# Twenty-eight transposes moved from TensorE to the DMA queue, and the whole order written anew, in a decoder layer

## The chip, the cores and the metric

The kernel runs on one core of a Trainium2 chip. The metric is the device time of one execution in microseconds (us), as the median of several runs.

## What is computed

The input is 16 batches of 128 tokens by 256 features. Three stages follow each other, and each ends in a residual sum and a layer norm:

```python
q  = (x @ W_q.T).reshape(B, S, H, hd);  kv = (x @ W_kv.T).reshape(B, S, H, hd)   # H = 16, hd = 16
qf, kvf = l2_normalize(fft(q)), l2_normalize(fft(kv))
values  = ifft(qf * cumsum(kvf, axis=1)).real @ W_o.T
x1 = layernorm(x + values)
x2 = layernorm(x1 + mha(x1, ctx, ctx))          # 16 heads, causal mask before the softmax
x_q = ternary(x2, 0.33, 0.5);  w = ternary(weight, 0.2, 0.6) + rram_variation
out = layernorm(x2 + x_q @ w.T)
```

## The kernel before

Every batch is one tile of 128 partitions (tokens), and all 16 go through the same steps. There is no loop: for each engine the whole program is written out as a list of calls, `step(batch)` or `step(batch, part)`, with waits on semaphores between them. Each engine works its list from top to bottom, so a step that has to wait holds everything behind it on its engine. Steps of up to six batches are mixed in a list. Tables at the top (`PROJ`, `CUM`, `APPROX`, `SCORES`, `OUT` and others) say in which of the eight PSUM banks each product of each batch lies. Most tiles have two buffers, taken by batch number modulo 2.

The steps of one batch, with the engine and the line that the profile gives:

- First stage. `project` (TensorE, L747) makes q and kv in the frequency domain; `square`, `log_norms`, `root_norms`, `square_roots` (ScalarE) and `sum_squares`, `half_step`, `refine_norms`, `unit_vectors` (VectorE) scale them to length one. `cumulate` (TensorE, L753) is the running sum. `straight_products`, `cross_products` (VectorE) and `y_real`, `y_imaginary` (GpSimd, L334, L339) multiply. `transpose_y` and `attend` (TensorE, L759, L767) end the stage.
- Every layer norm i of a batch: the residual sum with its total (`add_attention`, `add_cross_attention` L2028, `add_feed_forward` L2034), `negative_mean` (VectorE, L2040), `deviations` (ScalarE, L1449), `variance` and `root` (GpSimd, L344, L349), then the scaling (`normalise_x1` L2048, `normalise_x2` L2053 on VectorE, `result` for the third).
- Second stage. `round_x1` writes a bfloat16 copy of x1 (tile `x1_b`). `transpose_x1_b` (TensorE, L774) turns it into PSUM, four 128x128 pieces; `copy_x1T_b` brings it back to SBUF (tile `x1T_b`). `approximate` (TensorE, L785) makes rough scores from it, and `row_max` (VectorE, L2067, four parts c) takes their row maxima, which are written into a spare column of x1. Then `transpose_x1` (L792), `copy_x1T` (L1427), `score` (L802) make the exact scores with the maxima already subtracted, `exponentials` (ScalarE, L1431) and `mask` (GpSimd, L355) the weights, `weigh` (TensorE, L809, four parts c) the weighted sums, `copy_outT`, `transpose_out` (L816), `invert_sums`, `divide` (L2077) the result.
- Third stage. `ternary_above` and `ternary` (L2062) make the bfloat16 ternary input `xq`, `transpose_xq` (TensorE, L822) and `copy_xqT` turn it, `feed_forward` (L829) multiplies it with three bfloat16 parts of the weight.

Some steps have two forms, and the lists say for each batch which engine does it: `round_x1` is on ScalarE (L1419) for twelve batches and on VectorE (L1967) for four; `copy_x1T_b` is on ScalarE (L1423) for fifteen and on VectorE (L1971) for one; `copy_xqT` is on ScalarE (L1440) for fourteen and on VectorE (L1975) for two; `result` is on VectorE (L1979) for twelve and on ScalarE (L1444) for four, where it also needs `shift_of` (VectorE, L2044); `ternary_above` is on VectorE (L2058) for eleven and on GpSimd (L360) for five.

`score` and `approximate` use 32 rows of the TensorE array for one product and `weigh` 32 columns, so that several products lie in the array side by side (tiled products); all other products use the whole array. All loads and stores are issued by SyncE (SP) in one list.

## Time and profile before

| | |
|---|---|
| median of 3 runs | 160.67 us (160.65 to 160.75) |
| the profiled execution | 160.63 us, of which the span of the trace is 158.9 us |
| granted TensorE clock, mean over the span | 0.983 |

The profile gives for each engine the busy time within the span, the work that ended last as a chain followed back from the end, the idle time before an instruction and what ended it, and the instructions in order of time. Busy times of TensorE overlap with its own next instruction, so there the distance from one start to the next is the better measure.

### The profile page before, as it was taken

The numbers are of one execution on the slowest core, as the hardware profiler recorded it, in microseconds if no ns is written. First come the engines' busy times: TensorE is split into PE (matmuls) and PEld (weight loads), VectorE is DVE, ScalarE is ACT, GpSimd is POOL, SyncE is SP. The second block draws the span as 40 slices with busy tenths as digits, with TensorE's granted clock in tenths as the row PEclk, the third lists the DMA queues.
The fourth block names the chain that finished last, engine by engine and source line by source line (L and its number), as shares of the span: only waits on it lengthen the run. The fifth ranks groups of instructions, "written<-read, shape, count | busy, mean of one in ns | idle before, by whom it ended". The sixth has DMA issues, their size and how long they took to land.

```text
span 158.9 us, 4915 instructions
## 1 busy us (share of the span) xinstructions
PE 142.3 (90%) x1821; PEld 96.2 (61%) x1821; DVE 140.4 (88%) x428; ACT 117.5 (74%) x320; POOL 99.2 (62%) x210
## 2 busy tenths in 40 slices
PE   6999999999999999899999999987979899978450
PEld 2844566645777766468655767755747667865230
DVE  0148999999999998999989999999999899999872
ACT  3116566567996899956897898897968988988761
POOL 4000256141489178957777971999766998998742
PEclk9999999999999999999999999999999999999985
DMA  4968702398330123503058232032106011020222
GB/s 105 286 197 238 257 8 66 103 294 304 99 103 2 41 95 103 194 8 127 11 182 270 80 101 67 4 102 77 65 0 199 5 37 37 0 70 0 86 78 71
DMA packets 13624, 16.58 MB, mean 104 GB/s; under 512 B 1568, under 2 KB 9504, under 8 KB 13600
## 3 DMA queue, kind: packets, MB, share of 16 engines
q1 hardware_dynamic: 13600, 16.27, 32.5%
q8 instruction: 14, 0.23, 0.6%
q14 instruction: 10, 0.08, 0.2%
HBM read 14.16 MB, written 2.10 MB: 102 GB/s over the span
## 4 chain that ended last, share of the span: by engine, by line
DVE 42%; PE 30%; POOL 12%; ACT 8%; issue 5%; POOLq 0%; DVEq 0%
DVE x L2067 15%; PE p L747 13%; POOL rstd L349 5%; POOL probs L355 4%; PE p L767 3%; PE p L753 3%; DVE x L2048 3%; POOL ve L344 3%; ACT dev L1449 2%; ACT probs L1431 2%; DVE x L2053 2%; PE p L802 2%; PE p L718 2%; DVE xq L2062 2%; DVE r L2028 2%
## 5 line engine op out<-in xcount | busy, mean ns | idle before, releaser
L355 POOL TENSOR_SCALAR_AFFINE_SELECT probs<-probs 128x512 f32<-128x512 f32 x64 | 41.0, 659 | 4.9 <-ACT probs L1431 4.0
L2067 DVE TENSOR_REDUCE x<-p 128x4 f32<-128x512 f32 x64 | 41.2, 681 | 0.0
L1431 ACT ACTIVATE probs<-p 128x512 f32<-128x512 f32 x64 | 34.9, 603 | 4.8 <-PE p L802 4.8
L747 PE MATMUL p<-w_in,xT_s 128*128 128x512 f32 x64 | 30.2, 602 | 0.3 <-ACT w_in L1391 0.3
L349 POOL TENSOR_TENSOR rstd<-ve,power 128x1 f32<-128x1 f32 x48 | 28.2, 588 | 2.3
L1449 ACT ACTIVATE dev<-r,neg 128x256 f32<-128x256 f32 x48 | 24.3, 510 | 3.8 <-DVE neg L2040 3.2
L344 POOL TENSOR_SCALAR ve<-spread 128x1 f32<-128x1 f32 x48 | 11.1, 231 | 22.2 <-ACT dev L1449 19.4
L334 POOL TENSOR_TENSOR y<-y 128x112 f32<-128x112 f32 x16 | 6.8, 425 | 23.0 <-DVE y L2012 22.9
L802 PE MATMUL p<-x1T,keys 32*128 32x128 f32 x512 | 18.8, 283 | 2.4 <-DVE x L2067 1.7
L802 PEld LDWEIGHTS p<-x1T,keys 32*128 32x128 f32 x512 | 15.8, 186 | 7.4 <-issue 2.7
L809 PE MATMUL p<-probs,vals 128*32 128x128 f32 x512 | 19.8, 278 | 0.5 <-POOL probs L355 0.2
L747 PEld LDWEIGHTS p<-w_in,xT_s 128*128 128x128 f32 x64 | 11.5, 190 | 10.7 <-issue 9.9
L767 PE MATMUL p<-w_out,yT_s 128*128 128x256 f32 x64 | 17.0, 392 | 0.0
L809 PEld LDWEIGHTS p<-probs,vals 128*32 128x32 f32 x512 | 12.2, 109 | 6.2 <-issue 2.3
L1399 ACT ACTIVATE sq<-p 128x512 f32<-128x512 f32 x16 | 9.5, 596 | 8.7 <-PE p L747 8.7
L829 PE MATMUL p<-w_ffn,xqT_s 128*128 128x256 bf16 x96 | 13.2, 276 | 1.9 <-ACT xqT_s L1440 1.1
L767 PEld LDWEIGHTS p<-w_out,yT_s 128*128 128x128 f32 x64 | 11.2, 190 | 2.6 <-issue 0.9
L1984 DVE TENSOR_REDUCE ssq<-sq 128x32 f32<-128x512 f32 x16 | 10.9, 679 | 2.0 <-ACT sq L1399 2.0
L1436 ACT ACTIVATE outT_s<-p 128x512 f32<-128x512 f32 x16 | 9.5, 596 | 3.0 <-PE p L809 3.0
L829 PEld LDWEIGHTS p<-w_ffn,xqT_s 128*128 128x128 bf16 x96 | 8.4, 98 | 4.9 <-ACT xqT_s L1440 1.8
L2000 DVE TENSOR_TENSOR unit<-p,rnA 128x512 f32<-128x512 f32 x16 | 10.9, 681 | 0.1
L792 PE MATMUL p<-ident_s,x 128*128 128x128 f32 x64 | 10.2, 282 | 0.6 <-DVE x L2067 0.5
(75 smaller groups left out, 268.7 us busy)
## 6 DMA issues: line engine op xcount, KB each, us to landing
vals<-ctxV SPq DMA_DIRECT2D x16, 256.0 KB, 3.6
keys<-ctxK SPq DMA_DIRECT2D x16, 256.0 KB, 2.9
xT_s<-xT SPq DMA_DIRECT2D x16, 128.0 KB, 3.1
x_s<-x SPq DMA_DIRECT2D x16, 128.0 KB, 2.7
out<-res SPq DMA_DIRECT2D x16, 128.0 KB, 1.7
wq_s<-w_q SPq DMA_DIRECT2D x1, 256.0 KB, 2.7
wkv_s<-w_kv SPq DMA_DIRECT2D x1, 256.0 KB, 4.0
fw_s<-ffn_wT SPq DMA_DIRECT2D x1, 256.0 KB, 3.9
```

What stands on the lines that cost most here:

```text
L344: nc.gpsimd.tensor_scalar(ve[i][n % 2][:], spread[i][n % 2][:], 1.0 / DIM, LN_EPS, ALU.mult, ALU.add).then_inc(ve_done[i], 1)
L349: nc.gpsimd.tensor_tensor(rstd[i][n % 2][:], ve[i][n % 2][:], power[:], ALU.pow).then_inc(rstd_done[i], 1)
L355: nc.gpsimd.affine_select(out=part, in_=part, compare_op=ALU.is_ge, fill=0.0, base=0, pattern=[[0, GH], [1, TOK]], channel_multiplier=-1). ...
L747: last = nc.tensor.matmul(p[PROJ[n]][:], xT_s[n % XR][:, g, :], w_in[:, g, :], start=(g == 0), stop=(g == 1))
L767: last = nc.tensor.matmul(p[ATT[n]][:, 0:DIM], yT_s[n % 2][:, g, :], w_out[:, g, :], start=(g == 0), stop=(g == 1))
L802: last = nc.tensor.matmul(p[SCORES[n][s]][:, g * TOK:(g + 1) * TOK], keys[n % KV][slot, g, :], x1T[n % 2][slot, g, :], start=True, stop=True)
L809: last = nc.tensor.matmul(p_out(n)[SLOT * g:SLOT * (g + 1), c, :], vals[n % KV][:, GH * g + c, :], probs[n % 2][:, c, g, :], start=True, s ...
L829: last = nc.tensor.matmul(p[FFN[n]][:, 0:DIM], xqT_s[n % 2][:, g, :], w_ffn[i][:, g, :], start=(g == 0 and i == 0), stop=(g == 1 and i == 2))
L1431: nc.scalar.activation(probs[n % 2][:, c, :, :].rearrange("p g q -> p (g q)"), p[SCORES[n][c]][:], ACT.Exp, scale=HD ** -0.5).then_inc(exp ...
L1449: nc.scalar.activation(dev[i][n % 2][:], (r1, r2, r3)[i][n % 2][:], ACT.Square, bias=neg[i][n % 2][:], accum_out=spread[i][n % 2][:]).then ...
L1984: nc.vector.tensor_reduce(ssq[n % 2][:].rearrange("p (j h) -> p j h", j=2), sq[n % 2][:].rearrange("p (j h k) -> p j h k", j=2, h=HEADS), ...
L2067: nc.vector.tensor_reduce(x1[n % X1R][:, c::GH, HD], p[APPROX[n][c]][:].rearrange("p (h k) -> p h k", h=GH), AX.X, ALU.max, negate=True).t ...
```

## The change

- `transpose_x1_b` for all 16 batches and `transpose_xq` for batches 0 to 11 become DMA transposes from SBUF to SBUF, issued by SP. With them the 16 `copy_x1T_b` and twelve of the `copy_xqT` are gone. Batches 12 to 15 keep `transpose_xq` on TensorE, with `copy_xqT` on ScalarE.
- Each step with two forms now has one: `round_x1` and `result` on ScalarE, `ternary_above` on VectorE. All 16 `result` take a `shift_of` on VectorE.
- The lists of all five engines and the bank tables are written anew. Tiled products stand next to each other more often: the TensorE list has 34 stretches of tiled steps instead of 42.
- `transpose_out` writes its four pieces interleaved, so that `divide` reads heads in order. New switches (`HALVES`, `IN_PSUM`) stand at values that change nothing.

```diff
-XQT = (7, 4, 6, 3, 6, 4, 4, 7, 1, 1, 6, 2, 7, 3, 4, 5)
+XQT = (6, 6, 6, 6, 6, 6, 3, 6, 6, 6, 4, 6, 6, 4, 4, 4)
...
+            def transpose_x1_b(n):
+                sp.dma_start_transpose(x1T_b[n % 2][:], x1_b[n % 2][:].rearrange("p h s -> p (h s)")).then_inc(x1T_b_in[n % 2], 16)
+
+            def transpose_xq(n):
+                sp.dma_start_transpose(xqT_s[n % 2][:], xq[n % 2][:]).then_inc(xqT_in[n % 2], 16)
...
-            def ternary_above(n):
-
-                nc.gpsimd.tensor_scalar(above[n % 2][:], x2[n % 2][:], TH_X, None, ALU.is_gt).then_inc(above_done_pool, 1)
...
-            def transpose_x1_b(n):
-
-                for g in range(GROUPS):
-                    last = nc.tensor.transpose(tile16(X1BT[n], GROUPS, TOK)[:, g, :],
-                                               x1_b[n % 2][:, GH * g:GH * (g + 1), :].rearrange("p h s -> p (h s)"),
-                                               ident_b[:])
-                last.then_inc(x1T_b_done, 1)
...
-                    last = nc.tensor.transpose(p_out(n)[:, g, :], outT_s[n % 2][:, g, :], ident_s[:])
+                    last = nc.tensor.transpose(pv(n)[:, g::GH, :], outT_s[n % 2][:, g, :], ident_s[:])
...
-            def copy_x1T_b(n):
-
-                nc.scalar.activation(x1T_b[n % 2][:], tile16(X1BT[n], GROUPS, TOK), ACT.Copy).then_inc(x1T_b_copied, 1)
...
-                nc.scalar.activation(res[n % 2][:], r3[n % 2][:], ACT.Identity, bias=shift[2][n % 2][:],
+                nc.scalar.activation(heads(res[n % 2][:]), residual(n, 2), ACT.Identity, bias=shift[2][n % 2][:],
...
-            def round_x1(n):
-
-                nc.vector.tensor_copy(x1_b[n % 2][:, :, 0:HD], x1[n % X1R][:, :, 0:HD]).then_inc(x1_b_done_dve, 1)
...
-            def result(n):
-
-                nc.vector.tensor_scalar(res[n % 2][:], r3[n % 2][:], neg[2][n % 2][:],
-                                        rstd[2][n % 2][:], ALU.add, ALU.mult).then_inc(out_ready_dve, 1)
```

Three places show what the new lists do. The first is SP from the load of the first batch's `keys` to the fourth DMA transpose. Names are destination and source; before:

```order
L179 DMA keys<-ctxK 128x512
L173 DMA xT_s<-xT 128x256
L176 DMA x_s<-x 128x256 x2
L173 DMA xT_s<-xT 128x256
L176 DMA x_s<-x 128x256
L182 DMA vals<-ctxV 128x512
L173 DMA xT_s<-xT 128x256
L179 DMA keys<-ctxK 128x512 x4
```

and now, from the load of `keys` of batch 1 on:

```order
L199 DMA keys<-ctxK 128x512
L202 DMA vals<-ctxV 128x512
L199 DMA keys<-ctxK 128x512 x2
L211 DMA_TRANSPOSE x1T_b<-x_b 128x4x128 x2
L196 DMA x_s<-x 128x256 x2
L202 DMA vals<-ctxV 128x512 x2
L211 DMA_TRANSPOSE x1T_b<-x_b 128x4x128
L193 DMA xT_s<-xT 128x256
L211 DMA_TRANSPOSE x1T_b<-x_b 128x4x128
```

Each DMA transpose stands behind a wait for its own `round_x1`, so the loads behind it in SP's list now wait for that too.

The second place is TensorE around the weighing (`L809`, now `L865`) of batches 0 and 1. Before:

```order
L809 MATMUL p<-probs,vals 32x128 x4
L785 MATMUL p<-keys,x1T_b 128x128 x16
L809 MATMUL p<-probs,vals 32x128 x12
L774 MATMUL p<-ident_b,x_b 128x128 x4
L767 MATMUL p<-w_out,yT_s 128x256 x2
L816 MATMUL p<-ident_s,outT_s 128x128 x4
L759 MATMUL p<-ident_s,y 128x128 x2
L774 MATMUL p<-ident_b,x_b 128x128 x4
L785 MATMUL p<-keys,x1T_b 128x128 x16
L792 MATMUL p<-ident_s,x_2 128x128 x4
L809 MATMUL p<-probs,vals 32x128 x16
```

and now:

```order
L865 MATMUL p<-probs,vals 32x128 x16
L858 MATMUL p<-x1T,keys 128x128 x16
L872 MATMUL p<-ident_s,outT_s 128x4x32 x4
L811 MATMUL p<-w_in,xT_s 128x512 x2
L865 MATMUL p<-probs,vals 32x128 x16
L841 MATMUL p<-keys,x1T_b 128x128 x16
L823 MATMUL p<-ident_s,y 128x128 x2
```

The transposes of `x1_b` are gone from the list, and weighing stands whole and beside another tiled step (`L858` is `score`, `L841` `approximate`).

The third place is GpSimd from the first mask of batch 14 (its `probs` are buffer 0) to the last mask of batch 15 (`probs1`). Before (`ve1`, `rstd1` belong to the second layer norm, `ve2`, `rstd2` to the third):

```order
L355 AFFINE_SELECT probs0<-probs0 128x512
L349 TENSOR_TENSOR rstd1_0<-ve1_0,power 128x1
L355 AFFINE_SELECT probs0<-probs0 128x512
L344 TENSOR_SCALAR ve2_0<-spread2_0 128x1
L355 AFFINE_SELECT probs0<-probs0 128x512
L349 TENSOR_TENSOR rstd2_0<-ve2_0,power 128x1
L355 AFFINE_SELECT probs0<-probs0 128x512
L344 TENSOR_SCALAR ve1_1<-spread1_1 128x1
L349 TENSOR_TENSOR rstd1_1<-ve1_1,power 128x1
L355 AFFINE_SELECT probs1<-probs1 128x512 x2
L344 TENSOR_SCALAR ve1_0<-spread1_0 128x1
L349 TENSOR_TENSOR rstd1_0<-ve1_0,power 128x1
```

(then the last two masks), and now:

```order
L421 AFFINE_SELECT probs0<-probs0 128x512 x4
L410 TENSOR_SCALAR ve2_1<-spread2_1 128x1
L415 TENSOR_TENSOR rstd2_1<-ve2_1,power 128x1
L421 AFFINE_SELECT probs1<-probs1 128x512
L410 TENSOR_SCALAR ve1_0<-spread1_0 128x1
L415 TENSOR_TENSOR rstd1_0<-ve1_0,power 128x1
L421 AFFINE_SELECT probs1<-probs1 128x512 x3
```

From the first mask of batch 14 to the end of the program GpSimd has 13 `variance` and 14 `root` before and 11 of each now; the eight masks are in both.

## Rows read from the trace of the kernel before

**Rows 1.** The page: busy time, share and instructions of each engine

```profile
PE 142.3 (90%) x1821; PEld 96.2 (61%) x1821; DVE 140.4 (88%) x428; ACT 117.5 (74%) x320; POOL 99.2 (62%) x210
```

**Rows 2.** Stretches: length, busy PE, PEld, DVE, ACT, POOL, clock, DMA share, GB/s

```profile
24.00:135.60 111.60, 105.96 (x1549) 73.60 (x1548) 108.52 (x319) 91.73 (x247) 77.83 (x157) 1.00 0.31 99
135.60:158.90 23.30, 13.96 (x204) 9.58 (x202) 18.41 (x77) 15.94 (x45) 16.39 (x36) 0.88 0.15 52
```

**Rows 3.** The chain that ended last: shares from 135 us on; start, us, work

```profile
by line: POOL probs L355 22.0%; POOL rstd L349 21.1%; issue 15.2%; POOL ve L344 9.9%; DVE res L1979 3.4%; DVE r L2034 3.2%; DVE xq L2062 3.2%; PE p L829 2.8%; ACT dev L1449 2.5%; POOLq L66 2.5%; DVE above L2058 1.8%; DVE x L2053 1.6%; DVE n
...
127.79 1.79 DVE x L2067 x3
...
134.62 0.55 POOL rstd L349
...
148.88 0.56 POOL rstd L349
...
156.32 0.41 DVE res L1979
```

**Rows 4.** Groups of instructions that go or move: count, busy us, mean ns

```profile
L1979 DVE TENSOR_SCALAR res<-r,neg,rstd 128x256 f32<-128x256 f32 x12 | 6.1, 504 | 1.7 <-POOL rstd L349 1.7
L1967 DVE CAST x_b<-x 128x256 bf16<-128x256 f32 x4 | 1.6, 390 | 0.0
L1975 DVE COPY xqT_s<-p 128x256 bf16<-128x256 bf16 x2 | 0.6, 286 | 0.2 <-PE p L822 0.2
L1971 DVE COPY x1T_b<-p 128x512 bf16<-128x512 bf16 x1 | 0.4, 414 | 0.0
L2058 DVE TENSOR_SCALAR above<-x 128x256 bf16<-128x256 f32 x11 | 4.2, 378 | 0.0
L2044 DVE TENSOR_TENSOR shift<-neg,rstd 128x1 f32<-128x1 f32 x4 | 1.0, 244 | 0.4 <-POOL rstd L349 0.4
L1423 ACT ACTIVATE x1T_b<-p 128x512 bf16<-128x512 bf16 x15 | 9.0, 597 | 1.1 <-PE p L774 1.1
L1440 ACT ACTIVATE xqT_s<-p 128x256 bf16<-128x256 bf16 x14 | 5.4, 384 | 1.7 <-PE p L822 1.7
L1444 ACT ACTIVATE res<-r,shift,rstd 128x256 f32<-128x256 f32 x4 | 2.4, 594 | 0.3 <-DVE shift L2044 0.2
L1419 ACT ACTIVATE x_b<-x 128x256 bf16<-128x256 f32 x12 | 5.1, 422 | 1.3 <-DVE x L2048 1.3
L360 POOL TENSOR_SCALAR above<-x 128x256 bf16<-128x256 f32 x5 | 4.6, 918 | 1.7 <-DVE x L2053 1.4
```

**Rows 5.** TensorE in order of time: start, length, operation, shapes, count

```profile
95.64 0.39 PE L774 MATMUL p<-ident_b,x_b 128*128 128x128 bf16 x4
95.86 0.27 PE L822 MATMUL p<-ident_b,xq 128*128 128x128 bf16 x2
...
102.92 1.10 PE L809 MATMUL p<-probs,vals 128*32 128x128 f32 x32
...
106.36 0.43 PE L809 MATMUL p<-probs,vals 128*32 128x128 f32 x8
```

**Rows 6.** DMA issues: count, KB each, median us from issue to landing

```profile
vals<-ctxV SPq DMA_DIRECT2D x16, 256.0 KB, 3.6
...
out<-res SPq DMA_DIRECT2D x16, 128.0 KB, 1.7
```

**Rows 7.** GpSimd's operations: count, busy us, mean ns

```profile
L355 POOL TENSOR_SCALAR_AFFINE_SELECT probs<-probs 128x512 f32<-128x512 f32 x64 | 41.0, 659 | 4.9 <-ACT probs L1431 4.0
L349 POOL TENSOR_TENSOR rstd<-ve,power 128x1 f32<-128x1 f32 x48 | 28.2, 588 | 2.3
L344 POOL TENSOR_SCALAR ve<-spread 128x1 f32<-128x1 f32 x48 | 11.1, 231 | 22.2 <-ACT dev L1449 19.4
```

**Rows 8.** Batch 0 from its bfloat16 copy to its first rough scores

```profile
27.51 0.42 ACT L1419 ACTIVATE x_b<-x 128x256 bf16<-128x256 f32 x1
...
29.50 0.34 PE p L785 x15
```

More of the change, by code:

```diff
@@ L265, in _ @@
+            transpose_x1_b(8)
+            load_keys(10)
             load_x(13)
@@ L1682, in _ @@
-            copy_x1T_b(7)
-            act.wait_ge(neg_done[1], 4)
-            deviations(3, 1)
-            act.wait_ge(neg_done[0], 11)
-            deviations(10, 0)
+            act.wait_ge(shift_done[2], 2)
+            result(1)
+            copy_yT(12)
+            act.wait_ge(yT, 14)
+            copy_yT(13)
+            round_x1(9)
+            act.wait_ge(neg_done[1], 5)
+            deviations(4, 1)
             act.wait_ge(scored, 7)
             exponentials(6, 3)
+            exponentials(6, 0)
@@ new lines, in _ @@
+            dve.wait_ge(rden_done, 3)
+            divide(2)
+            unit_vectors(11)
+            dve.wait_ge(above_done, 2)
+            ternary(1)
+            dve.wait_ge(att_done, 3)
+            add_cross_attention(2)
+            dve.wait_ge(approx, 5)
+            row_max(4, 0)
+            row_max(4, 1)
+            row_max(4, 2)
+            row_max(4, 3)
+            dve.wait_ge(squared, 13)
+            sum_squares(12)
+            dve.wait_ge(added[1], 3)
+            negative_mean(2, 1)
@@ L2436, in _ @@
-            divide(5)
-            dve.wait_ge(rstd_done[2], 3)
-            shift_of(2, 2)
+            dve.wait_ge(above_done, 4)
+            ternary(3)
+            cross_products(13)
+            dve.wait_ge(squared, 16)
+            sum_squares(15)
+            dve.wait_ge(yT, 13)
+            straight_products(14)
+            dve.wait_ge(approx, 8)
+            row_max(7, 0)
+            cross_products(14)
+            row_max(7, 2)
+            dve.wait_ge(rstd_done[2], 2)
+            shift_of(1, 2)
@@ L2583, in _ @@
             normalise_x2(8)
-            divide(9)
-            negative_mean(6, 2)
             dve.wait_ge(att_done, 10)
             add_cross_attention(9)
-            row_max(13, 1)
-            round_x1(14)
-            dve.wait_ge(xqT, 8)
-            copy_xqT(7)
-            dve.wait_ge(rstd_done[0], 16)
+            dve.wait_ge(x2_done, 9)
+            ternary_above(8)
+            dve.wait_ge(approx, 14)
+            row_max(13, 2)
             dve.wait_ge(added[1], 10)
+            negative_mean(9, 1)
@@ L2602, in _ @@
-            ternary(8)
-            dve.wait_ge(rstd_done[2], 6)
-            dve.wait_ge(stored[1], 32)
-            result(5)
+            dve.wait_ge(rstd_done[2], 7)
+            shift_of(6, 2)
+            dve.wait_ge(added[2], 8)
+            negative_mean(7, 2)
+            dve.wait_ge(att_done, 11)
+            add_cross_attention(10)
+            normalise_x2(9)
             dve.wait_ge(approx, 15)
             row_max(14, 0)
-            row_max(14, 2)
-            row_max(14, 1)
-            add_cross_attention(10)
@@ L2611, in _ @@
-            dve.wait_ge(x1T_b_done, 16)
-            copy_x1T_b(15)
-            row_max(14, 3)
-            dve.wait_ge(ffn, 8)
-            add_feed_forward(7)
+            dve.wait_ge(added[1], 11)
+            negative_mean(10, 1)
+            row_max(14, 1)
+            dve.wait_ge(x2_done, 10)
+            ternary_above(9)
+            row_max(14, 2)
+            dve.wait_ge(above_done, 10)
+            ternary(9)
             dve.wait_ge(out_done, 12)
             invert_sums(11)
+            row_max(14, 3)
@@ L2637, in _ @@
-            ternary(9)
-            dve.wait_ge(added[2], 9)
-            negative_mean(8, 2)
+            dve.wait_ge(x2_done, 11)
+            ternary_above(10)
+            row_max(15, 3)
+            dve.wait_ge(above_done, 11)
+            ternary(10)
+            dve.wait_ge(ffn, 10)
+            add_feed_forward(9)
+            dve.wait_ge(added[2], 10)
+            dve.wait_ge(rstd_done[1], 12)
+            normalise_x2(11)
+            negative_mean(9, 2)
+            dve.wait_ge(x2_done, 12)
@@ L2640, in _ @@
+            ternary_above(11)
+            dve.wait_ge(above_done, 12)
+            ternary(11)
             dve.wait_ge(out_done, 13)
             invert_sums(12)
[L2642 removed]
+            dve.wait_ge(rstd_done[2], 9)
+            shift_of(8, 2)
             dve.wait_ge(rden_done, 13)
             divide(12)
[L2645 to L2649 removed]
```

2778 lines of the change are left out of this document (1361 added, 1417 removed).

## The prediction

> **What bounds the kernel now.** I read four views, in this order. The page's busy times first: VectorE has 140.4 of 158.9 us, ScalarE 117.5, GpSimd 99.2 [rows 1]. Then the stretches. From 24 to 135.6 us, that is up to the end of the last `row_max` of batch 15, VectorE is busy 108.5 of 111.6 us: it stands idle for only 3.1 us there, so this stretch lasts as long as VectorE's list lasts. TensorE is busy nearly as long (106.0), ScalarE (91.7) and GpSimd (77.8) less [rows 2]. After that come 23.3 us in which no engine is full: VectorE 18.4, GpSimd 16.4, ScalarE 15.9 [rows 2]. Third, the chain of waits says who leads there: from 134.62 to the end of the `root` at 148.88 the chain lies on GpSimd without a break, mask, variance and root in turn, and of all from 135 us on the three GpSimd lines have 22, 21 and 10%, with 15% of "issue" between them [rows 3]. So there are two regimes: VectorE's list, then GpSimd's list, and at the end the latency of the last layer norms. Fourth, the groups of instructions give the prices.
>
> **VectorE.** Gone: 12 `result` (504 ns), 4 `round_x1` (390), 2 `copy_xqT` (286), 1 `copy_x1T_b` (414) [rows 4]: 6.05 + 1.56 + 0.57 + 0.41 = 8.6 us. Added: 5 `ternary_above` (378) = 1.9 us, and 12 `shift_of` (244) = 2.9 us [rows 4]. Net 3.8 us less. `divide` and `transpose_out` only change the order of addresses; I cost that at nothing.
>
> How these 3.8 us lie matters. In the new list 7 `result` fewer stand behind the last `row_max` of batch 15, and 6 `shift_of` more; one step fewer of each of `add_feed_forward`, `add_cross_attention`, `normalise_x2`, `ternary_above`, `ternary` and `copy_xqT`, and two `negative_mean`. With the prices above and 0.4 us for a step of 256 elements (0.41 for the last `result` [rows 3]) this is 3.5 + 2.3 - 1.5 = 4.3 us less behind that point, and so 0.5 us more ahead of it. The head thus grows by 0.5 us through VectorE's own work.
>
> **ScalarE and GpSimd.** ScalarE loses 15 `copy_x1T_b` (597) and ten `copy_xqT` (384), 12.8 us, and gets 12 `result` (594) and 4 `round_x1` (422), 8.8 us: 4.0 us less [rows 4]. GpSimd loses five `ternary_above` (918), 4.6 us [rows 4], all ahead of the masks of batch 11.
>
> **TensorE.** Four transposes of `x1_b` take from 95.64 to 95.86 = 0.22 us of its time [rows 5], two of `xq` half of that by count; 16 and 12 of them make 3.5 + 1.3 = 4.8 us less. Tiled stretches fall from 42 to 34. A weighing of one part (8 matmuls) takes 0.43 us, one of four parts (32) takes 1.10 us [rows 5], so (1.10 - 0.43) / 24 x 8 = 0.22 us is work and 0.2 us is the cost of starting a stretch: eight stretches fewer are worth at most 1.6 us. Together some 5 to 6 us of 142. The Trainium skill (TensorEngine Tiling (Array Packing), Tiling Modes) says that changing the tiling mode drains the array, which agrees in kind with that 0.2 us.
>
> None of these three is the bound of the head; what they can shorten is its 3.1 us of VectorE idle time [rows 2]. Between nothing and all of it I take 1.0 us, since most of the chain there already lies on VectorE.
>
> **The DMA transposes.** The trace of before has none. What they must beat is slack, so I count it. Before, batch 0's rounded copy ends at 27.93 us and the first rough scores start at 29.50: 1.6 us for turn, copy and waits [rows 8]. In the new lists, the VectorE work between `normalise_x1` of a batch and the first `row_max` that needs its rough scores is, at the durations above and 0.6 us for each step of 512 elements (1.79 us for three `row_max` [rows 3]), about 5.7 us for batches 0 to 2, 7.9 for batch 3, and 9 to 19 for all others. Rounding (0.42), rough scores (0.4) and handing over take about 1.1 of it, which leaves 4.6 us from issue to landing for the first three. Between `ternary` and `add_feed_forward` lie 5.4 to 8.9 us for batches 0 to 9 and 4.0 and 4.2 for batches 10 and 11; less 1.0 for the products and handing over, 3.0 us at the tightest.
>
> The nearest rows are plain transfers: 128 KB out of SBUF land in 1.7 us, 256 KB in 3.6 us [rows 6]; a transposed copy of x1 moves 128 KB, of xq 64 KB. Lower bound 1.7 us, upper bound for the same bytes twice the larger, 7 us, since a transfer of two-byte elements need not keep the pace. I take 3 us. Then all is hidden behind VectorE's work and the term is nothing. Per microsecond above 4.6 the start slips by one, and the tight batches of the third stage with it.
>
> The Trainium skill (VectorE: DVE Perf Modes, The three transpose paths) speaks against this change: 1309 ns by DMA against 390 ns on TensorE for 128x128, and TensorE where a PSUM destination will do. Estimated from that page, four pieces one after the other would be 5.2 us for x1 and two 2.6 us for xq: by it the start would slip by about 1 us with the fixed latency on top, by the rows by nothing. No row here shows such a transfer.
>
> SP now waits for 28 further signals in one list. Behind a waiting transpose stand loads for batches that come two or more later, and stores; a late store holds a `result` of two batches later, and that now holds the exponentials on ScalarE behind it. I cost this at nothing: results are needed by nobody else, and the signals come in the order in which SP waits.
>
> **The tail.** GpSimd's list from the first mask of batch 14 on has 3 `root` and 2 `variance` fewer: 3 x 0.59 + 2 x 0.23 = 2.2 us by the means [rows 7], and 0.3 us of issue between them. VectorE's list is 4.3 us shorter there. ScalarE has six `result` more (3.6) but two `deviations` and two copies less (2.2). As the chain is GpSimd's, I take its 2.5 us as the floor and 4.3 us as the ceiling, and choose 3.0 us. At the very end the scaling of batch 15 was one VectorE instruction of 0.41 us at 156.32 [rows 3]; now it is `shift_of` and a ScalarE `result` of 0.59 [rows 4]: 0.4 us more.
>
> **The sum.** +0.5 (head, VectorE) - 1.0 (idle in the head) - 3.0 (tail) + 0.4 (last scaling) = -3.1 us against the profiled execution of 160.6 us, which is the median of the runs within 0.1 us: 157.5 us. The ends of the terms give 154.1 (all idle of the head, the tail at its ceiling: 0.5 - 3.1 - 4.3 + 0.4 = -6.5) and 159.0 (nothing in the head, the floor in the tail: 0.5 - 2.5 + 0.4 = -1.6).
>
> **The rivals.**
>
> Transposes are late (slower). If a transposed copy takes 6.5 us from issue to landing, the start slips by 1.9 us, and batches 0, 5, 9, 10 and 11 of the third stage each stop VectorE for 1 to 3 us: some 7 to 8 us in all against 3.1 won, 165 us. It decides from about 5.5 us on. For it: two-byte elements, and the page above. Against it: 28 transfers of 2.9 MB in all on DMA engines that are busy for 31% of the head [rows 2], and 9 us and more of slack in 12 of 16 batches. Chance 0.14.
>
> New waits in the new lists. The old lists leave VectorE only 3.1 us idle in 111.6 [rows 2]; a new order with other banks may stop it more often. If it is idle for 6.5 us instead, the gain is gone and the time is 161.5 us. For it: everything is in another place, and every wait on a bank is new. Against it: more slack at each step. Chance 0.13.
>
> The tail gives nothing, since ScalarE with six more `result` takes GpSimd's place: 0.5 - 1.0 + 0.4, 160.5 us. ScalarE is busy 15.9 of 23.3 us there now [rows 2] and would get 1.4 more. Chance 0.07.
>
> More than forecast: the head's idle time goes nearly whole and the tail follows VectorE: 154.1 to 155.7 us. For it: every engine's list gets shorter. Against it: the first waits of a list are latency, not load. Chance 0.16.
>
> The forecast itself, 155.8 to 159.3 us, has 0.50.
>
> **How the numbers follow.** Within 0.2%, 160.35 to 161.0 us, is about what a measurement of this kernel tells from no change. Faster: 0.50 + 0.16, and 0.02 of the second rival: 0.68. Same: 0.07. Slower: 0.14 + 0.11 = 0.25. The range leaves out the deepest part of the good case and the upper half of the bad one: 154.3 to 163.0 us.
>
> **What would show it right or wrong.** VectorE's busy time at 136.6 us, ScalarE's at 113.5, GpSimd's at 94.6. From issue to landing of a DMA transpose about 3 us, and no wait of `approximate` or `feed_forward` on a transfer above 1 us in total. VectorE idle between 24 us and the last `row_max` of batch 15 at 3 us or less, with that `row_max` ending at 134 to 136 us, and 20 to 21 us from there to the end. The prediction is wrong if the rows of the DMA transposes show more than 4.6 us, if the waits name them, or if VectorE's idle time in the head has doubled.

## The result, and the profile after

The changed kernel takes 159.29 us (median of 11 executions, 158.59 to 161.84); the kernel before, run beside it, takes 160.67 (160.62 to 160.93). The ratio is 0.9921 with a 95% interval of 0.9898 to 0.9944: 0.8% less, where the forecast was 157.5 us, 2% less. The executions of the changed kernel lie much further apart than those of the kernel before. Medians here and below are over all executions, while the ratios leave out the disturbed ones (the worst, of the kernel before, took 227 us) and lie near the ratio of the means, so the two need not match.

The page of the changed kernel, part 1 (busy times) and part 3 (the DMA queue that SP feeds: packets, MB, share of 16 engines):

```profile
PE 136.1 (86%) x1733; PEld 91.1 (58%) x1733; DVE 136.9 (87%) x426; ACT 114.5 (73%) x311; POOL 94.9 (60%) x205
...
q1 hardware_dynamic: 25760, 19.15, 46.9%
```

The work went where the price list said [rows 1]: VectorE 136.9 us (forecast 136.6), ScalarE 114.5 (113.5), GpSimd 94.9 (94.6). So the loads of the whole span were foreseen and the time was not. The stretches of the changed kernel, cut at the same two places as [rows 2]:

```profile
24.00:135.60 111.60, 100.93 (x1471) 69.76 (x1469) 108.92 (x324) 87.53 (x239) 74.28 (x154) 1.00 0.49 118
135.60:157.60 22.00, 12.72 (x189) 8.53 (x188) 15.08 (x65) 16.51 (x44) 14.04 (x31) 0.95 0.18 56
```

The last `row_max` of batch 15 ends at 135.55 us, 0.1 us earlier than before; VectorE's idle time up to there is still 2.7 us. The rest of the gain is the tail, 22.0 instead of 23.3 us. In it no engine is near full: ScalarE 16.5, VectorE 15.1, GpSimd 14.0. GpSimd has 2.4 us less than before there and VectorE 3.3 (forecast 2.2 and 4.3), and the tail is 1.2 us shorter. The chain of waits in the tail, with shares by line from 135 us on, and its last 13 us piece by piece (start, us, what):

```profile
by line: PE p L885 13.8%; DVE xq L2048 8.2%; ACT probs L1442 6.7%; PE p L872 5.8%; DVE r L2020 5.3%; ACT res L1455 5.2%; ACT xqT_s L1451 5.1%; ACT outT_s L1447 4.8%; PE p L865 4.5%; ACT dev L1460 4.3%; issue 4.0%; DVE above L2044 3.5%; PE p
...
143.04 1.03 PE p L865 x24
144.09 0.61 ACT outT_s L1447
...
144.74 0.67 PE p L872 x4
...
150.91 0.13 PE p L878 x2
151.06 0.39 ACT xqT_s L1451
...
151.50 0.84 PE p L885 x6
152.37 0.44 DVE r L2020 x2
152.83 0.16 DVE neg L2026
153.02 0.61 ACT dev L1460 x2
...
153.70 0.19 POOL ve L410
...
153.94 0.60 POOLq L75
154.56 0.17 DVE shift L2030
154.75 0.60 ACT res L1455
```

Before, three GpSimd lines led this stretch [rows 3]; now no line has more than 14%, and GpSimd is nearly absent. Read it from the bottom: scaling, shift, root, variance, deviations, mean, sum, product, copy, turn. That is one batch going through all engines, with hardly a gap between one step and the next. From the end of the last weighing of batch 15 (144.02 us) to the end of the span it lasts 13.6 us; in the kernel before that weighing ended at 145.00, and the same way lasted 13.9. The change shortened this part by 0.3 us only; the other 0.9 us lie ahead of that end of weighing (9.35 us from the last `row_max` before, 8.5 now).

Neither part is batch 15's own work alone. ScalarE has three steps of other batches between batch 15's scores and its last exponentials:

```profile
138.61 0.60 ACT L1455 ACTIVATE res<-r,shift,rstd 128x256 f32<-128x256 f32 x1 [0.46 <-DVE shift L2030]
...
139.62 0.51 ACT L1460 ACTIVATE dev<-r,neg 128x256 f32<-128x256 f32 x1
...
141.08 0.59 ACT L1447 ACTIVATE outT_s<-p 128x512 f32<-128x512 f32 x1
141.56 0.60 ACT L1442 ACTIVATE probs<-p 128x512 f32<-128x512 f32 x1
```

And from 146.15 to 150.91 us, left out above, the chain of waits runs through the third stages of batches 13 and 14 (two `feed_forward` of 0.83 us each, at 147.30 and 150.08), beside the second layer norm of batch 15.

The DMA transposes. For tile `x1T_b`, and then for `xqT_s`, the view of the tile gives the fastest, median and slowest time from issue to landing:

```profile
DMA to landing us min/median/max: 2.4/2.7/5.5
```

```profile
DMA to landing us min/median/max: 2.3/3.6/4.9
```

SP's list of the changed kernel ahead of the first `xqT_s` (start, us that the issue took), and from its waits the weight loads of TensorE that waited for one (us, times, longest):

```profile
57.56 0.58 SPq L202 DMA_DIRECT2D vals<-ctxV  x1
58.19 0.43 SPq L199 DMA_DIRECT2D keys<-ctxK  x1
58.66 0.44 SPq L196 DMA_DIRECT2D x_s<-x  x1
59.14 0.43 SPq L193 DMA_DIRECT2D xT_s<-xT  x1
59.61 0.43 SPq L199 DMA_DIRECT2D keys<-ctxK  x1
60.52 1.18 SPq L214 DMA_TRANSPOSE xqT_s<-xq  x1
```

```profile
PEld p L885 <- DMA xqT_s<-xq: 1.9, 2, 1.4
```

A typical transfer keeps inside its slack. But the first `xqT_s`, issued at 60.52 behind five loads, landed 4.9 us later, and `feed_forward` of batch 0 stood before it. TensorE works its list in order, so what stood behind that product was late too.

### The profile page after: what moved, and what is told of

Its sections match the earlier page's. It is cut to its first block, busy times and chain, and to the rows that moved or that the text cites. A ratio compares the mean times of both kernels' runs of the same rounds, so it can differ in the third digit from the quotient of the medians.

```text
span 157.6 us, 4753 instructions
## 1 busy us (share of the span) xinstructions
PE 136.1 (86%) x1733; PEld 91.1 (58%) x1733; DVE 136.9 (87%) x426; ACT 114.5 (73%) x311; POOL 94.9 (60%) x205
## 3 DMA queue, kind: packets, MB, share of 16 engines
q1 hardware_dynamic: 25760, 19.15, 46.9%
## 4 chain that ended last, share of the span: by engine, by line
PE 44%; DVE 41%; ACT 7%; issue 3%; DMA 3%; POOLq 0%; POOL 0%
DVE x L2053 12%; PE p L811 11%; PE p L831 7%; PE p L858 5%; PE p L885 4%; PE p L817 4%; DMA xqT_s<-xq 3%; DVE xq L2048 3%; PE p L865 2%; ACT probs L1442 2%; DVE x L2034 2%; DVE above L2044 2%; DVE x L2039 2%; PE p L782 2%; DVE r L2020 2%
## 5 line engine op out<-in xcount | busy, mean ns | idle before, releaser
L421 POOL TENSOR_SCALAR_AFFINE_SELECT probs<-probs 128x512 f32<-128x512 f32 x64 | 41.7, 668 | 10.9 <-ACT probs L1442 10.1
L2053 DVE TENSOR_REDUCE x<-p 128x4 f32<-128x512 f32 x64 | 41.7, 676 | 0.8 <-PE p L841 0.6
L1442 ACT ACTIVATE probs<-p 128x512 f32<-128x512 f32 x64 | 34.3, 600 | 5.3 <-PE p L858 5.1
L410 POOL TENSOR_SCALAR ve<-spread 128x1 f32<-128x1 f32 x48 | 9.8, 205 | 22.9 <-ACT dev L1460 20.4
L858 PE MATMUL p<-x1T,keys 32*128 32x128 f32 x512 | 19.2, 283 | 4.5 <-DVE x L2053 1.8
L858 PEld LDWEIGHTS p<-x1T,keys 32*128 32x128 f32 x512 | 16.1, 186 | 9.2 <-DVE x L2053 3.3
L865 PE MATMUL p<-probs,vals 128*32 128x128 f32 x512 | 18.9, 277 | 0.8 <-ACT yT_s L1430 0.5
L831 PE MATMUL p<-w_out,yT_s 128*128 128x256 f32 x64 | 16.5, 388 | 0.6 <-DVE x L2053 0.6
L865 PEld LDWEIGHTS p<-probs,vals 128*32 128x32 f32 x512 | 12.5, 109 | 6.0 <-issue 2.4
L400 POOL TENSOR_TENSOR y<-y 128x112 f32<-128x112 f32 x16 | 7.1, 444 | 14.0 <-DVE y L1998 13.9
L872 PE MATMUL p<-ident_s,outT_s 128*128 128x128 f32 x64 | 10.2, 282 | 1.0 <-ACT outT_s L1447 1.0
```

Source lines behind the costliest of these rows:

```text
L421: nc.gpsimd.affine_select(out=part, in_=part, compare_op=ALU.is_ge, fill=0.0, base=0, pattern=[[0, GH], [1, TOK]], channel_multiplier=-1). ...
L831: last = nc.tensor.matmul(p[ATT[n]][:, 0:DIM], yT_s[n % 2][:, g, :], w_out[:, g, :], start=(g == 0), stop=(g == 1))
L858: last = nc.tensor.matmul(p[SCORES[n][s]][:, g * TOK:(g + 1) * TOK], keys[n % KV][slot, g, :], x1T[n % 2][slot, g, :], start=True, stop=True)
L865: last = nc.tensor.matmul(p_out(n)[SLOT * g:SLOT * (g + 1), c, :], vals[n % KV][:, GH * g + c, :], probs[n % 2][:, c, g, :], start=True, s ...
L872: last = nc.tensor.transpose(pv(n)[:, g::GH, :], outT_s[n % 2][:, g, :], ident_s[:])
L1442: nc.scalar.activation(probs[n % 2][:, c, :, :].rearrange("p g q -> p (g q)"), p[SCORES[n][c]][:], ACT.Exp, scale=HD ** -0.5).then_inc(exp ...
```

## The experiments

Three numbers are taken from each profiled run. **Start**: first copy of `w_in` on VectorE. **Head**: from there to the end of the last `row_max` of batch 15. **Tail**: from there to the end of the span. "Products" are the last two `feed_forward`, which take 0.83 us each at a granted clock of 1.00 (2.4 GHz) and 1.46 at 0.50 (1.2 GHz); before, they stand as one group of twelve matmuls, which takes 1.47 us at 1.00. The span is shown to 0.1 us, so the tails are good to 0.05. Start, head, tail and products are those of one execution each.

| run | median us | ratio to before, 95% | start | head | tail | products |
|---|---|---|---|---|---|---|
| before | 160.67 | | 6.99 | 128.66 | 23.25 | 1.69 |
| after | 159.29 | 0.9921 (0.9898-0.9944) | 6.84 | 128.71 | 22.05 | 0.83, 0.83 |
| e1 no xq by DMA | 159.59 | 0.9928 (0.9902-0.9953) | 6.71 | 127.68 | 23.51 | 1.46, 1.46 |
| e2 no x1 by DMA | 160.36 | 0.9943 (0.9916-0.9971) | 7.21 | 128.10 | 23.39 | 1.46, 1.46 |
| e3 neither | 160.31 | 0.9954 (0.9925-0.9982) | 7.17 | 128.15 | 23.38 | 1.46, 1.46 |
| e4 results on VectorE | 161.39 | 1.0002 (0.9973-1.0030) | 7.58 | 130.28 | 22.64 | 0.83, 1.46 |
| f1 filler | 158.80 | 0.9905 (0.9868-0.9941) | 6.82 | 127.97 | 22.01 | 0.83, 0.83 |
| f2 batch 15 first | 160.69 | 0.9937 (0.9917-0.9957) | 7.29 | 128.52 | 23.89 | 1.46, 1.46 |
| f3 f1 + f2 | 159.66 | 0.9930 (0.9904-0.9955) | 7.32 | 129.29 | 22.59 | 0.83, 0.83 |
| f4 e3 + f1 | 158.84 | 0.9907 (0.9873-0.9941) | 6.97 | 128.16 | 21.97 | 0.83, 0.83 |
| g1 f1, short results | 159.02 | 0.9901 (0.9881-0.9921) | 6.66 | 128.29 | 21.95 | 0.83, 0.83 |
| g2 f1, idle on chain | 160.57 | 0.9989 (0.9966-1.0012) | 7.29 | 128.73 | 23.18 | 0.83, 0.83 |
| g3 f1, idle off chain | 159.00 | 0.9874 (0.9846-0.9901) | 7.24 | 128.00 | 21.96 | 0.83, 0.83 |
| g4 f1, SP order | 158.75 | 0.9874 (0.9861-0.9887) | 7.37 | 127.68 | 22.05 | 0.83, 0.83 |
| k1 before, narrow masks | 159.99 | 0.9971 (0.9954-0.9988) | 6.43 | 128.65 | 23.72 | 2.75 |
| k2 g4, narrow masks | 158.93 | 0.9881 (0.9864-0.9897) | 7.17 | 129.00 | 21.83 | 0.83, 0.83 |
| k3 SP order alone | 159.83 | 0.9932 (0.9907-0.9956) | 6.97 | 129.58 | 22.55 | 0.83, 1.38 |
| k4 before + filler | 159.99 | 0.9961 (0.9947-0.9974) | 6.29 | 128.62 | 23.29 | 1.47 |
| n1 before again | 160.81 | 0.9996 (0.9986-1.0007) | 6.04 | 128.69 | 24.37 | 2.77 |
| n2 after again | 159.46 | 0.9911 (0.9877-0.9944) | 7.10 | 128.25 | 22.65 | 0.83, 1.46 |

### What the transfers cost, and who leads the tail

Theory A was that the DMA transposes took back what the head should gain; theory B that ScalarE took GpSimd's place in the tail; theory C that the new order has waits of its own. In e1 to e3 the transfers and the waits for them go, and SP keeps its waits:

```diff
-            transpose_xq(0)          # e1, e3: all 12
-            transpose_x1_b(0)        # e2, e3: all 16
-            pe.wait_ge(xqT_in[0], 16)
-            pe.wait_ge(x1T_b_in[0], 16)
+            for tile in xqT_s: nc.gpsimd.memset(tile[:], 0.0)
```

> The changed kernel without the twelve DMA transposes of the ternary inputs and without TensorE's waits for them; xqT_s holds zeros, so the product of the third stage is left out of the result for batches 0 to 11 (its instructions all run). SP keeps its waits for the ternary inputs, so the order of the loads stays. Theory A (the DMA transposes took back what the head was to gain: late landings, 1.2 us of SP each, crowded DMA engines): the waits of L885 on a transfer (2.7 us before them) go and the time falls by 1 to 2 us, to 157.3 to 158.3. Theory B (the tail's six more scalings on ScalarE are what is missing): no more than 0.3 us of change, 159.0 to 159.6. Theory C (the new written order has its own chain of waits, whatever the DMA does): no more than 0.3 us either.

> The changed kernel without the sixteen DMA transposes of x1_b and without the waits for them; x1T_b holds zeros, so the rough scores and their maxima are zero (all instructions run, the exact scores are then shifted by nothing). SP keeps its waits for round_x1. Theory A: in the trace of the changed kernel no x1 transpose is waited for over 0.5 us, so the direct wait is worth nothing, but the DMA engines are freed of 13 us of work in the stretch where xq's and the loads crowd: 0.3 to 1 us less, 158.3 to 159.0. Theories B and C: 159.0 to 159.6.

> Both left out: no DMA transpose in the program. Theory A: the sum of the two, 156.8 to 158, and the spread from run to run (1 % for the changed kernel, 0.2 % for the one before) goes back to that of before. Theories B and C: 159.0 to 159.6, with the spread as it is.

In e4 `result` of batches 8 to 15 goes back to VectorE:

```diff
-            shift_of(8, 2)           # VectorE, 8 to 15
+            result(8)
-            result(8)                # ScalarE, 8 to 15
```

> The changed kernel with the last scaling of batches 8 to 15 on VectorE again (504 ns there instead of a shift_of of 244 ns and 594 ns on ScalarE). Theory B (ScalarE, busy 16.5 of the last 22.0 us, took the place of GpSimd as what leads the tail): ScalarE is freed of 0.6 us per batch from 135 us on, VectorE pays 0.26 us per batch: 0.5 to 1.5 us less, 157.8 to 158.8. Theory A: no gain, 0.3 us slower or so, since VectorE gets 2.1 us more work: 159.3 to 160. Theory C: within 0.5 us either way.

No median came out under that of the changed kernel. Theory A in its strong form fell: without any DMA transpose the time is no lower. So did B: e4 is slower, and its tail, less the 0.63 us of one slow product, is the same 22.0 us. Its head is what grew. C's bound of 0.3 us holds for e1 alone; e2 and e3 are 1.0 us above the changed kernel, and no run tests the order by itself. TensorE in e4, around 123 us (start, us, line, shapes, idle before and its releaser), and the stretches there:

```profile
122.75 0.41 PE L841 MATMUL p<-keys,x1T_b 32*128 32x128 bf16 x16 [1.19 <-DMA x1T_b<-x_b]
...
124.08 2.09 PE L858 MATMUL p<-x1T,keys 32*128 32x128 f32 x32
```

```profile
122.00:124.00 2.00, 1.25 (x32) 0.87 (x32) 1.45 (x7) 0.33 (x1) 0.84 (x2) 0.79 0.63 155
124.00:126.00 2.00, 2.00 (x36) 1.80 (x32) 1.87 (x5) 1.57 (x5) 0.56 (x2) 0.50 0.99 282
```

One late transfer stopped TensorE for 1.2 us, the granted clock fell to 0.50 right behind, and 32 scoring matmuls took 2.09 us instead of 1.17. The fall is not shown to come from the stop: in k3, further down, the same transfer stops TensorE as long, and the clock stays at 1.00:

```profile
122.28 0.41 PE L841 MATMUL p<-keys,x1T_b 32*128 32x128 bf16 x16 [1.24 <-DMA x1T_b<-x_b]
...
123.49 1.17 PE L858 MATMUL p<-x1T,keys 32*128 32x128 f32 x32 [0.22 <-DVE x L2053]
```

Why the other executions of e4 were slow as well, its one trace does not tell.

What e1 to e3 did show lies in two columns. Their heads are 127.7 to 128.2 us; no wait for a transfer is left in e1 and e3, and one of 0.8 us in e2. And their tails are 1.3 to 1.5 us longer, because the clock fell earlier: the two products alone take 1.26 us more. TensorE in e1's tail, then one stretch of e1 and the same of the changed kernel (the granted clock is the third number from the right):

```profile
146.15 0.83 PE L875 MATMUL p<-w_ffn,xqT_s 128*128 128x256 bf16 x6 [0.48 <-ACT xqT_s L1429]
...
149.03 1.46 PE L875 MATMUL p<-w_ffn,xqT_s 128*128 128x256 bf16 x6 [0.47 <-ACT xqT_s L1429]
...
151.18 1.46 PE L875 MATMUL p<-w_ffn,xqT_s 128*128 128x256 bf16 x6 [0.48 <-ACT xqT_s L1429]
```

```profile
148.00:150.00 2.00, 1.36 (x7) 0.85 (x8) 1.36 (x6) 1.33 (x4) 1.58 (x5) 0.55 0.03 4
```

```profile
148.00:150.00 2.00, 0.42 (x4) 0.11 (x2) 1.78 (x7) 1.67 (x7) 1.44 (x4) 1.00 0.22 70
```

The profile of the changed kernel had happened to keep its clock. Over the 58 executions of the changed kernel and its variants without filler (after, n2, e1 to e3, k3), the 11 with a mean clock of 0.99 or more have a median of 158.67 us, the 25 below 0.973 one of 160.27, and the 22 between one of 159.78.

### Holding the clock, and moving the queue in front of batch 15

f1 puts 15 matmuls of zeros into a free bank ahead of TensorE's waits in the last 16 us; f2 moves three steps behind those of batch 15; f3 does both; f4 is f1 without DMA transposes:

```diff
+            busy(7, 2)               # f1: seven such places, 15 in all
             pe.wait_ge(outT_copied, 16)
-            result(8)                # f2, ScalarE: ahead of exponentials(15, 0)
             exponentials(15, 1)
+            result(8)
-            result(11)
             deviations(15, 1)
+            result(11)
-            shift_of(12, 2)          # f2, VectorE
             ternary(15)
+            shift_of(12, 2)
```

> The changed kernel with 15 idle matmuls (zeros, 512 columns, into a bank that nothing reads, 0.21 us each at full clock) on TensorE in the gaps of the last 16 us, ahead of its waits. Clock theory (in the records of the changed kernel and of its variants the granted clock falls to half at 147 to 155 us, and where it falls early the last products of batches 14 and 15 take 1.46 instead of 0.83 us each; runs at a mean clock of 0.994 took 158.6 to 158.8 us, those at 0.970 160.0 to 160.5): the clock stays up until the last product, the median falls to 158.6 to 159.0 and the spread from run to run shrinks to under 1 us. Rival (the clock is only a symptom, the spread comes from the DMA transposes): the median stays at 159.3 to 159.6, or rises by up to 0.5 us with what the idle matmuls hold up.

> The changed kernel with three steps moved behind those of batch 15 in the tail: on ScalarE result(8) behind the third part of the exponentials of batch 15 and result(11) behind its deviations, on VectorE shift_of(12) behind its ternary. No engine gets or loses work. Chain theory (the tail is the chain of batch 15 through all engines, and lasts 22.0 us from the last row_max in both the changed kernel and the one with eight scalings back on VectorE): each move takes its delay off the chain, 0.5 + 0.5 + 0.2 = 1.2 us, so 158.1, and 0.6 at least (158.7) where the next wait takes half of it. Rival (an engine's total bounds the tail: GpSimd as the prediction had it, or ScalarE, busy 16.5 of 22.0 us): no more than 0.2 us of change, 159.1 to 159.5.

> Both edits together. If the clock theory and the chain theory hold, they add: 157.3 to 157.9 us, with a spread under 1 us. If only one holds, the time is that of the one alone.

> The idle matmuls in the kernel without any DMA transpose (zeros in xqT_s for batches 0 to 11 and in x1T_b for all: the third stage's product and the rough scores are left out of the result). In the first four experiments a lower clock in the tail may have hidden what the transfers cost. With the clock held, the difference to the changed kernel with the idle matmuls is the price of the 28 DMA transposes: by the forecast's term nothing (within 0.2 us of it, 158.5 to 159.0), by the trace without xq's transfers, where the last row_max ended 1.2 us earlier, 0.5 to 1.2 us less (157.6 to 158.3).

f1's median is 0.5 us lower, as the clock theory said, and the clock is 0.993 or more in all its executions. But they still lie between 158.3 and 160.6 us: the clock is not the whole spread. f4 equals f1 within 0.1 us: with the clock held, the 28 transfers cost nothing in the median, nor in f1's profile (head 127.97 against 128.16). Nor does the spread go with them: f4, without any, lies between 158.4 and 160.5 us. f2 and f3 failed: the tail did not lose 1.2 us but grew by 0.6. ScalarE in f3 shows why:

```profile
138.61 0.60 ACT L1454 ACTIVATE outT_s<-p 128x512 f32<-128x512 f32 x1
139.72 0.60 ACT L1449 ACTIVATE probs<-p 128x512 f32<-128x512 f32 x1 [0.51 <-PE p L858]
140.68 0.51 ACT L1467 ACTIVATE dev<-r,neg 128x256 f32<-128x256 f32 x1 [0.36 <-DVE neg L2033]
...
141.18 1.06 ACT L1449 ACTIVATE probs<-p 128x512 f32<-128x512 f32 x2
142.14 0.60 ACT L1462 ACTIVATE res<-r,shift,rstd 128x256 f32<-128x256 f32 x1
```

`result(8)` had stood mostly in a gap, since the scores of batch 15 were not ready. Moved, it left the gap empty, and the next `add_feed_forward` on VectorE then waited for it (0.41 us), a later one for `result(11)` (0.44). The expectation of the chain theory (158.1, at most 158.7 us) failed: a step that stands ahead of batch 15's can't be moved away for nothing, because other batches' steps hang on it.

### Load or chain: ScalarE

g1 shortens six `result` to one column; g2 and g3 add the same four idle copies on ScalarE, in one piece ahead of batch 15's deviations or spread over four gaps. All on top of f1. g4 changes SP's list:

```diff
-            result(8)                # g1, 8 to 13: 1 column of 256
+            short_result(8)
+            idle(0, 1, 2, 3)         # g2
             act.wait_ge(neg_done[1], 16)
+            idle(2)                  # g3: one ahead of each of four waits
             act.wait_ge(neg_done[2], 16)
-            load_keys(6)             # g4, SP: these four stood here
-            load_x(12); load_xT(15); load_keys(7)
             transpose_xq(0)
+            load_keys(6)
             transpose_xq(1)
+            load_x(12); load_xT(15); load_keys(7)
```

> The changed kernel with the idle matmuls of the first filler run (they hold the clock) and with result(8) to result(13) on ScalarE over one column instead of 256; the other 255 columns of the output of batches 8 to 13 are not computed. ScalarE has about 0.4 us less for each, 2.4 us less of its 16.5 in the tail. If ScalarE's total bounds the tail (it took GpSimd's place), the tail from the last row_max falls from 22.0 to about 20, and the time by 1.5 to 2.4 us. If the tail is the dependency chain of batch 15, only what stood directly ahead of its steps counts (result(8) ahead of its exponentials, result(11) ahead of its deviations): 21.2 to 21.7, and the time falls by 0.3 to 0.8 us.

> The same filler kernel with four idle copies of 128x256 (0.3 to 0.4 us each, nothing reads them) on ScalarE directly ahead of the deviations of batch 15. Chain theory: their 1.2 to 1.5 us come in full on top of the tail, less the 0.1 us or so that ScalarE had to spare there: tail 23.1 to 23.5. Load theory: what the next experiment adds, and no more, since both add the same work.

> The same four idle copies on ScalarE, one each ahead of four waits of the tail in which ScalarE sat idle for 0.44 to 0.53 us (ahead of copy_outT(15), copy_xqT(13), deviations(15) of the third stage and result(15)). Chain theory: 0 to 0.2 us, tail 22.0 to 22.2, time that of the filler kernel (158.5 to 159.0). Load theory: as much as the run before.

> The filler kernel with SP's list changed at one place: load_keys(6), load_x(12), load_xT(15) and load_keys(7), which stood ahead of the first two transposes of ternary inputs, stand behind them (keys(6) between the two). In the profiled runs in which the head was late, the first xqT_s landed 4.9 us after its issue behind five loads, and TensorE waited up to 1.7 us for it at 65 us. If that queue is what the head loses in some executions, the wait is gone, the last row_max ends 127.5 to 128.2 us after the first copy of w_in in every profile, the slowest executions go and the median falls by 0.2 to 0.5 us against the filler kernel, to 158.4 or so. If the lateness comes from the transposes themselves, it moves to another transfer and the median stays at 158.8 with its spread.

The idle copies in g2 and one of those in g3:

```profile
148.11 1.32 ACT L1415 ACTIVATE dump<-warm 128x256 bf16<-128x256 bf16 x4
149.33 0.50 ACT L1473 ACTIVATE dev<-r,neg 128x256 f32<-128x256 f32 x1
```

```profile
146.02 0.41 ACT L1415 ACTIVATE dump<-warm 128x256 bf16<-128x256 bf16 x1
146.56 0.38 ACT L1464 ACTIVATE xqT_s<-p 128x256 bf16<-128x256 bf16 x1
```

In g2 they hold the deviations up by 149.33 - 148.11 = 1.22 us, and the tail is 1.17 us longer than f1's (23.18 against 22.01). In g3 the same work leaves it at 21.96. In g1 six scalings shortened by 0.2 us each leave it at 21.95. So ScalarE's load in the tail is worth nothing, up or down; work added in batch 15's chain is worth its full length. But work taken out of that chain was worth nothing: by the chain theory g1's tail should have fallen to 21.2 to 21.7 us, since `result(8)` and `result(11)` stand directly ahead of batch 15's steps. Its last weighing ends 8.5 us behind the last `row_max`, as in f1. Something else, nearly as long, holds the tail as soon as this chain gets shorter.

g4's head (127.68) is as short as e1's, the shortest, and its four executions lie between 158.54 and 158.80.

### GpSimd, the queue alone, and both kernels again

```diff
-            mask(14, 0)              # k1 in the kernel before, k2 in g4; parts 0 to 3
+            narrow_mask(14, 0)       # one of four head groups
```

> The kernel before with the four masks of batch 14 over 128x128 instead of 128x512 elements (three of four head groups of that batch are not masked, so its output is another). GpSimd has 1.1 to 1.8 us less in the tail, all of it ahead of batch 15's root, and was busy there without a gap. GpSimd bounds and then the chain of batch 15: the tail falls from 23.3 to between 22.0 and 22.5, the time to 159.5 to 160.0. GpSimd's load alone bounds it: the full 1.1 to 1.8 us, 158.9 to 159.6. GpSimd did not bound: within 0.3 us of 160.67.

> The best kernel so far (idle matmuls and SP's new order) with the same four masks of batch 14 narrowed. The tail is 22.0 us there. Batch 15's chain bounds: tail 21.7 to 22.0, time within 0.3 us of 158.75. GpSimd still bounds: 1.1 to 1.8 us less.

> The changed kernel with SP's new order and without the idle matmuls. The wait at 65 us on xqT_s is gone, but the clock can fall from 147 us on and make the last two products 0.63 us longer each: a median between 158.8 and 160.2, runs at a mean clock of 0.99 at 158.7 and those at 0.97 at 160.0. Against the run with both edits (158.75) this gives the clock's share, against the changed kernel (159.3) the queue's.

k4 has the filler in the kernel before (`busy(6, n)` ahead of five waits, 15 in all), n1 and n2 are the two kernels unchanged.

> The kernel before with 15 idle matmuls on TensorE in its gaps of 146.5 to 152 us. There the clock fell at 152 us in the profile, with the last product all but done, and its times don't follow the mean clock (160.59 at 0.994, 160.56 at 0.978): within 0.2 us of 160.67. If the lower clock costs it as much as the changed kernel, 0.5 us less.

> The kernel before, unchanged, as a second sample. If the start is a matter of the execution: the first copy of w_in anywhere from 6.3 to 7.6 us in the trace and the median 160.67 within 0.2. If it is a matter of the build: start and median may both stand off by up to 0.7 us.

> The changed kernel, unchanged, as a second sample with a second trace. Median 159.3 within 0.4; the tail in the trace is 22.0 us where the last two products take 0.83 us each and 23.4 where both take 1.46; the head (first copy of w_in to the end of the last row_max) 127.7 to 129.3 us, above 128.2 only where a wait on x1T_b or xqT_s is in the trace.

A narrow mask takes 0.29 us where a full one takes 0.64, so GpSimd has 1.4 us less. In the kernel before the tail is 23.72 us with products that took 2.75 instead of 1.47: 22.4 at full clock, against 23.25 - 0.22 = 23.0 without the edit, or 23.3 by k4, whose products ran at full clock. That is 0.6 to 0.9 of 1.4 us. In the changed kernel it gives 22.05 - 21.83 = 0.2. GpSimd did lead before, and after 0.6 to 0.9 us of relief something else does; which step of which engine, no run isolates, since neither VectorE nor TensorE was relieved.

k3 did not confirm g4: its profile has no wait at 65 us, but the one of 1.24 us on `x1T_b` at 122 us shown above, and its median is above that of the changed kernel. The lateness moves to another transfer. That SP's order helps is not shown; g4's quiet sample is four executions.

k4 went against what I expected: 0.7 us off the kernel before. n1 suggests why. TensorE's first work in n1 and in the first profile of the kernel before, and in n1 the last product:

```profile
4.20 1.06 PE L723 MATMUL p<-dft_s,wq_s 128*128 128x128 f32 x8
5.29 1.16 PE L723 MATMUL p<-dft_s,wkv_s 128*128 128x128 f32 x8
...
151.52 2.77 PE L829 MATMUL p<-w_ffn,xqT_s 128*128 128x256 bf16 x12
```

```profile
4.20 1.92 PE L723 MATMUL p<-dft_s,wq_s 128*128 128x128 f32 x8
5.91 1.49 PE L723 MATMUL p<-dft_s,wkv_s 128*128 128x128 f32 x8
```

The same instructions took 1.06 us in one execution and 1.92 in the other, from the same start. The execution that was fast early (start 6.04) was slow late (2.77), the other the other way round (6.99 and 1.69), and the two sums agree within 0.2 us. That would explain why the kernel before looks so steady, and why idle matmuls, which keep the end fast, help it by 0.7 us too. It rests on two traces and is not shown: in k4's own profile the tail is as long as before (23.29 against 23.25), and the gain lies in its early start (6.29), which the idle matmuls can't have caused.

## Why the prediction was wrong

**The loads of the whole span were right.** So was the price of going to ScalarE at the end: from the end of the last `root` to the end of the last scaling it is now 154.53 to 155.35, 0.82 us, against 156.28 to 156.73 before: 0.4 us more.

**The failed step is the tail's: "As the chain is GpSimd's, I take its 2.5 us as the floor and 4.3 us as the ceiling, and choose 3.0 us."** It measured 1.0 to 1.2 us with the last scaling in it, where the forecast had 3.0 - 0.4 = 2.6. GpSimd's shorter list was taken for time won, at its full length and with VectorE's relief on top. A chain that lies on one engine says that this engine leads now; it says nothing of what comes second, and the second was near. k1 and k2 show it: 1.4 us less on GpSimd is worth 0.6 to 0.9 before and 0.2 after. So the 2.5 us taken as the floor was none. g1 and g3 rule out ScalarE's total, e4 a move of it to VectorE, and g2 shows that a delay ahead of batch 15's step passes on to the end whole.

What comes second stays open. The way of the last batch through all engines is part of it: 13.6 of the tail's 22.0 us are that way behind its last weighing, and it lasted 13.9 in the trace of before. But this length would not have warned me: 23.3 - 13.9 leaves 9.4 us, room enough for 3.0. And it holds waits behind other batches' steps, which f2 and g1 did not turn into time. The change has other loads, other engines and another order at once, and no run gives each one's share of the 1.2 us.

**The head.** Forecast: 0.5 us less (+0.5 - 1.0). In seven profiles, without a wait for a transfer (e1, e3, f4) or with none above 0.8 us (e2, f1, g3, g4), it is 127.7 to 128.2 us, against 128.6 to 128.7 in four profiles of the kernel before and its variants: 0.5 to 1.0 less, as forecast or better. With late transfers it was 128.7 in the changed kernel's profile, 129.3 in f3, 129.6 in k3, and the gain is gone. The waits do not explain all: g1, with one of 1.5 us, has 128.3, and f2, g2 and k2, with none above 0.6, have 128.5 to 129.0. So the term **"all is hidden behind VectorE's work and the term is nothing"** holds for the median landing (2.7 and 3.6 us; I took 3), and not for the slowest ones. The first `xqT_s` landed after 4.9 us against a slack of 5.4 less 1.0. The slowest `x1T_b`, 5.5 us, was batch 14's, to which the forecast gave 9 to 19 us of VectorE's work to hide behind. There a second term failed, SP's list with its 28 further signals (**"I cost this at nothing"**): batch 14's copy of x1 was ready at 119.63 us, SP issued the transpose at 121.39, it landed at 126.88, and `approximate` started at 126.97. In k3 batch 13's was ready at 114.85, issued at 116.70 behind a store and a load, and landed at 122.03, 7.2 us after it was ready:

```profile
114.94 1.24 SPq L205 DMA_DIRECT2D out<-res  x1
116.22 0.43 SPq L199 DMA_DIRECT2D keys<-ctxK  x1
116.70 1.20 SPq L211 DMA_TRANSPOSE x1T_b<-x_b  x1
```

One such transfer stops TensorE for 0.3 to 1.7 us, and which it is changes from run to run. In the medians with the clock held (f1 against f4) all this is worth nothing. The Trainium skill (VectorE: DVE Perf Modes, The three transpose paths) would have made the two landings, as an estimate from its figures, 5.2 and 2.6 us; the medians were 2.7 and 3.6, so here the measurement decides.

**The clock** is no price of the change: held up in both kernels, it gives 158.80 against 159.99, a difference of 1.2 us, about the 1.2 to 1.4 that the two have without filler. It widened the spread of the changed kernel and hid in e1 to e3 what the transfers cost.

The sum as measured: head 0 to 0.5 us, tail 1.0 to 1.2, together about the 1.4 us of the medians. Of the 1.8 us that the forecast was too low, 1.4 to 1.6 lie in the tail and most of the rest in the head. Of the rivals, that ScalarE takes GpSimd's place was wrong in its mechanism; that the transposes are late was right in kind and far too large in price, since a wait of 1 us once is not a wait in five batches.

Open stays what holds the tail once GpSimd is relieved, why e4's executions are slow as a whole, why TensorE's first matmuls take longer in some executions, what spreads the executions with the clock held, and whether SP's order is worth anything. The fastest version run is g4 (idle matmuls and SP's order), 158.75 us, ratio 0.9874 (0.9861 to 0.9887): faster than before, and with its interval below that of the changed kernel's, on four executions; most of the difference is the idle matmuls' (f1, f4, g1 and g3 have 158.8 to 159.0).

## What to carry to other kernels

Before relief on the leading engine of a tail is booked as time, take some of its work away in the kernel before and measure: narrower masks took 1.4 us off GpSimd and 0.6 to 0.9 us off the tail, and in the changed kernel 0.2. The work taken off one engine is a ceiling for what its relief gives, not a floor. To learn whether an engine's load or its place in a chain counts, add the same idle work once in its gaps and once ahead of the last batch's step. That tells what a delay costs; what a relief gives is another question, and needs work taken away (g2 cost 1.2 us, g1 gave nothing). A transfer whose median fits its slack still stops an in-order engine where the slowest does not fit, so compare slack with the worst landing behind the longest queue, and count the time that the transfer waits to be issued.
